# Moving low parts, normalised tiles, sums of results and one set of routed rows from VectorE to GpSimd in a network-attention-network kernel

## What is computed

```python
x = x + 0.5 * ffn(layernorm(x), gate_w, expert_bias, w1, w2, w3)
x = x + attn(layernorm(x), Wq, Wk, Wv, Wo)      # 16 heads of 8, 256 x 256 scores, no mask
x = x + 0.5 * ffn(layernorm(x), gate_w, expert_bias, w1, w2, w3)

def ffn(x, ...):                                  # 8 experts, hidden 352, the best 2 of each token
    scores = softmax(xf @ gate_w.T); _, sel = top_k(scores + expert_bias, 2)
    routed = xf[token_idx] * top_scores_sorted[:, None]       # sorted by expert
    h = silu(routed @ w1[e]) * (routed @ w3[e]); out = h @ w2[e]
    return zeros.at[token_idx].add(out)
```

## Time and profile before

| | us |
|---|---|
| median of 3 runs | 738.89 (738.53 to 741.27) |
| the profiled execution, its own time | 737.8 |
| its span, first to last instruction | 736.0 |
| first network, to the first unit of attention | 0 to about 245 |
| batches 0 to 3 of the attention, from the residual in unit (0, 2) | 248.29 to 317.96 |
| batches 4 to 11, the same way | 317.96 to 441.47 |
| to the last maxima | 471.55 |
| to the first product of the second network | 507.97 |
| second network | to 736 |

### The profile page before, as it was taken

One profiled execution on the slowest core, in us unless ns is written; L12 is line 12 of the kernel. 1 busy time (PEld: TensorE's weight loads), 2 busy tenths in 40 slices (PEclk: granted clock), 3 DMA queues, 4 the chain that ended last, 5 costly groups with the idle time before them and its releaser, 6 DMA issues.

```text
span 736.0 us, 14989 instructions
## 1 busy us (share of the span) xinstructions
PE 621.3 (84%) x5080; PEld 475.7 (65%) x5080; DVE 446.4 (61%) x1164; ACT 390.6 (53%) x912; POOL 303.1 (41%) x312
## 2 busy tenths in 40 slices
PE   6399999999979778899899998899999999999100
PEld 6388999988857434455554554456989899999100
DVE  6955733235456989899999999973676322233211
ACT  1625764444422577778777787783457544444000
POOL 6067714565433373044000010005566077776474
PEclk9999999999999899999999999989999999999655
DMA  8358978787982454435334443016678878887322
GB/s 263 100 165 222 252 225 237 224 239 207 286 231 81 153 147 148 125 117 166 110 116 139 125 130 103 3 58 198 179 211 249 228 218 245 246 250 208 100 78 64
DMA packets 116586, 126.02 MB, mean 171 GB/s; under 512 B 12512, under 2 KB 99168, under 8 KB 116384
## 3 DMA queue, kind: packets, MB, share of 16 engines
q1 hardware_dynamic: 98544, 101.20, 45.7%
q0 software_dynamic: 9088, 18.63, 10.2%
q10 hardware_dynamic: 8880, 5.25, 2.3%
HBM read 89.37 MB, written 35.39 MB: 170 GB/s over the span
## 4 chain that ended last, share of the span: by engine, by line
PE 53%; DVE 24%; issue 6%; DMA 6%; POOL 5%; ACT 4%; SPq 1%; POOLq 0%; ACTq 0%; DVEq 0%
PE banks L684 13%; DVE mx L816 10%; PE banks L656 9%; PE banks L672 8%; PE banks L665 8%; POOL rows L588 4%; PE banks L1128 4%; PE banks L646 2%; PE banks L471 2%; ACT PT L1143 2%; DMA WR<-in_experts 2%; PE banks L1012 2%; PE banks L1101 1%; DVE resid L803 1%; DVE split L809 1%
## 5 line engine op out<-in xcount | busy, mean ns | idle before, releaser
L568 POOL DMA_INDIRECT xe<-routed_rows,idx x156 | 151.6, 972 | 224.7 <-PE banks L646 85.7
L816 DVE TENSOR_REDUCE mx<-banks 128x2 f32<-128x512 f32 x256 | 163.4, 683 | 8.9 <-PE banks L1103 7.7
L1143 ACT ACTIVATE PT<-banks 128x512 f32<-128x512 f32 x256 | 140.5, 604 | 36.4 <-PE banks L1114 34.1
L588 POOL DMA_INDIRECT rows<-slots_out,slot x128 | 124.0, 969 | 72.2 <-issue 27.8
L737 DVE TENSOR_TENSOR hidT<-banks,act 96x256 f32<-96x256 f32 (+1 forms) x92 | 34.9, 380 | 188.2 <-ACT act L718 187.9
L684 PE MATMUL banks<-WR,hidT 128*128 128x128 f32 x936 | 119.8, 275 | 0.6 <-ACT ye L727 0.6
L684 PEld LDWEIGHTS banks<-WR,hidT 128*128 128x128 f32 x936 | 111.9, 191 | 2.9 <-issue 1.0
L656 PE MATMUL banks<-xeT,WR 128*128 128x256 f32 (+1 forms) x368 | 86.1, 356 | 8.0 <-issue 3.8
L672 PE MATMUL banks<-xeT,WR 128*128 128x256 f32 (+1 forms) x368 | 82.8, 347 | 0.0
L665 PE MATMUL banks<-xeT,WR 128*96 128x256 f32 (+1 forms) x368 | 82.5, 347 | 0.0
L1128 PE MATMUL banks<-PT,V 128*32 128x256 f32 x1024 | 73.4, 407 | 4.5 <-ACT oT L1190 3.8
(11 more groups left out here) (160 smaller groups left out, 894.9 us busy)
## 6 DMA issues: line engine op xcount, KB each, us to landing
WR<-in_experts SPq DMA_DIRECT2D x92, 544.0 KB
stacks<-split SPq DMA_DIRECT2D x32, 384.0 KB
slots_out<-ye SPq DMA_DIRECT2D x156, 64.0 KB
QS<-stacks SPq DMA_DIRECT2D x64, 112.0 KB
KS<-stacks SPq DMA_DIRECT2D x64, 112.0 KB
routed_rows<-xn ACTq DMA_DIRECT2D x16, 256.0 KB, 5.3
routed_rows<-xn SPq DMA_DIRECT2D x12, 256.0 KB, 2.3
xe<-routed_rows,idx POOLq DMA_INDIRECT x156, 4.4
```

Source lines behind the costliest of these rows:

```text
L568: eng.indirect_dma_start(xe[:, i % XR, a, :], None, routed_rows[h], bass.IndirectOffsetOnAxis(ap=idx[h][:, tile:tile + 1], axis=0))\
L588: eng.indirect_dma_start(rows[:, k, t, :], None, slots_out[h], bass.IndirectOffsetOnAxis(ap=slot[h][:, k, t:t + 1], axis=0))\
L816: eng.tensor_reduce(mx[:, :, e, pair], maxima_bank(f)[:, :].rearrange("p (q n) -> p q n", q=2), AX.X, ALU.max).then_inc(s_max, 1)
L1143: eng.activation(PT[:, u % 4, 1 - k].rearrange("p t n -> p (t n)"), PS[f % 3], ACT.Exp, scale=scale).then_inc(s_exp2, 1)
```

## The change

Six edits. First, `split_low` for batches 3 to 15 and `normed_pair` for batches 4 to 15 are issued on POOL, in a new function `attention_gpsimd` that follows the units and waits on the exponentials in units 0, 3 and 5. Second, the six sums of results that fall in the attention (chunks 2 and 3 of the first group, all four of the second) are made on POOL (`combine_gpsimd`, two additions of 128x512); DVE keeps their statistics and waits for the sums. Third, the factor 0.5 moves from the sum to ACT's copy of the expert result `ye`, so that a sum is two plain additions on either engine. Fourth, POOL's gathers are issued from the same units and some of them later, the power after two of them. Fifth, the rows for the second choice are made on POOL (`rows_gpsimd`) once the attention's POOL work is done. Sixth, SP stores first- and second-choice rows in turns. A count `s_ready` tells POOL when a reciprocal root is ready.

```diff
-        def rows_vector(eng):
+        def rows_gpsimd(eng):
             eng.wait_ge(s_coef, 2 * 3)
             eng.wait_ge(s_comb, GC * HALVES)
             for t in range(TH):
                 eng.tensor_scalar(rows[:, 1, t, :], X[:, t, :], factor[:, 1, t:t + 1], offset[:, 1, t:t + 1],
                                   ALU.mult, ALU.add).then_inc(s_xv, 1)
-            for k, c in ((0, 0), (0, 1), (0, 2), (1, 0), (0, 3), (1, 1), (1, 2), (1, 3)):
+            for k, c in ((0, 0), (1, 0), (0, 1), (1, 1), (0, 2), (1, 2), (1, 3), (0, 3)):
...
+        def combine_gpsimd(eng, h, c):
+            per = TH // GC
+            eng.wait_ge(s_gath[h][c], 16 * TOP_K * per)
+            eng.wait_ge(s_comb, GC * h + c)
+            a, b = (rows[:, k, c * per:(c + 1) * per, :] for k in range(TOP_K))
+            xc = X[:, h * TH + c * per:h * TH + (c + 1) * per, :]
+            eng.tensor_tensor(a, a, b, ALU.add).then_inc(s_pair, 1)
+            eng.wait_ge(s_pair, GC * h + c - 1)
+            eng.tensor_tensor(xc, a, xc, ALU.add).then_inc(s_comb, 1)
...
-                    eng.copy(ye[:, r, 0:w, :].rearrange("p a d -> p (a d)"), PS[1][:, 0:w * D]).then_inc(s_ye, 1)
+                    eng.activation(ye[:, r, 0:w, :].rearrange("p a d -> p (a d)"), PS[1][:, 0:w * D], ACT.Copy,
+                                   scale=0.5).then_inc(s_ye, 1)
...
+        def attention_gpsimd(eng, *sides):
+            for n in range(BATCH):
+                for u in range(PAIRS):
+                    if u == 2 and n + 3 < BATCH:
+                        split_low(eng, n + 3)
+                    if u == 6 and n + 4 < BATCH:
+                        eng.wait_ge(s_ready, (3, 4, 5, 5, 6, 6)[n // 2])
+                        normed_pair(eng, n + 4)
+                    if u in (0, 3, 5):
+                        wait(eng, s_exp2, 2 * (PAIRS * n + u))
+                    aside(sides, PAIRS * n + u)
+        def first_results(eng, outs):
+            combine_gpsimd(eng, 0, 2)
+            yield
+            next(outs)
+            yield
+            root_gpsimd(eng, 4, 0, tiles_of_chunks(2))
+            for _ in outs:
+                yield
+            combine_gpsimd(eng, 0, 3)
+            yield
+            root_gpsimd(eng, 5, 0, tiles_of_chunks(3))
+            yield
...
+            attention_gpsimd(pool, (first_results(pool, outs), spans((0, 7, 1), (11, 11, 1)), 12),
+                             (second_results(pool), spans((13, 30, 1), (31, 31, 1), (36, 52, 1), (61, 61, 1)), 62),
+                             (third_root(pool), in_loads(90, 1), 90))
+            rows_gpsimd(pool)
...
-            attention_vector(dve, (finish(dve, 4, 0, 2), lambda i: 2 * int(2 <= i <= 4), 5),
-                             (finish(dve, 5, 0, 3), spans((8, 9, 1), (12, 13, 1), (20, 20, 2)), 2 * PAIRS + 5),
+            attention_vector(dve, (finish(dve, 4, 0, 2), spans((1, 3, 1), (4, 4, 2)), 5),
+                             (finish(dve, 5, 0, 3), spans((9, 11, 1), (12, 12, 2)), PAIRS + 5),
```

More of the change, by code:

```diff
@@ L227, in build @@
         s_wa, s_vzero = sem("s_wa"), sem("s_vzero")
+        s_ready, s_pair = sem("s_ready"), sem("s_pair")
         chain = [0]
@@ L261, in norm_sums, with norm_root @@
             yield
-        def norm_root(eng, n, h, t, rstd):
+        def norm_root(eng, n, h, t, rstd, ready=0):
             yield
@@ L270, in norm_root @@
             link(eng, eng.scalar_tensor_tensor(rr[:, t], rr[:, t], -0.5, var[h][:, t], ALU.mult, ALU.mult))
-            link(eng, eng.scalar_tensor_tensor(rstd, rr[:, t], 1.5, rough[h][:, t], ALU.add, ALU.mult))
+            last = eng.scalar_tensor_tensor(rstd, rr[:, t], 1.5, rough[h][:, t], ALU.add, ALU.mult)
+            if ready:
+                last.then_inc(s_ready, 1)
+                eng.wait_ge(s_ready, ready)
+            else:
+                link(eng, last)
             yield
@@ L287, in finish @@
             yield from norm_sums(eng, h, t, amean[:, tiles])
-            yield from norm_root(eng, n, h, t, arstd[:, tiles])
+            yield from norm_root(eng, n, h, t, arstd[:, tiles], n - 1)
         def tiles_of_chunks(*chunks):
@@ L1214, in attention_vector @@
                             largest(eng, f)
-                    if u == 2 and ahead:
-                        split_low(eng, n + 3)
                     if u == 2 and nxt:
```

50 lines of the change are left out of this document (24 added, 26 removed).

## The result

The changed kernel takes 744.21 us (median of 7 runs, 740.79 to 745.49); the kernel before takes 738.89 beside it (7 runs, 734.61 to 741.78). The ratio is 1.0083, 95% interval 1.0047 to 1.0119: slower by some 6 us where 9.4 less were forecast. The profiled execution took 740.79, the shortest of the seven; its span is 739.0, 3.0 longer than before. The stage that the change is about lost more than that. PE had waited there for expert weights in before (1.5 and 1.2 us, at 203.8 and 208.9); in after no such wait between 185 and 237 is over 0.6.

What follows compares the result with a forecast made beforehand. DVE and PE, both nearly full in the attention batches and feeding each other, were taken as the bound. Terms -1.3 + 1.1 + 1.4 + 1.6 + 5.9 + 0.6 + 0.1 gave 9.4 us less, 729.5 from 738.89; range 722.5 to 736.

Steps and rivals of the forecast that it cites:

- Batches 4 to 11: Quiet attention batches: each falls from 15.44 to 14.7 us as work leaves DVE, a gain of 5.9 us.
- The 0.39 behind the low part goes: Unit 2 of a batch: PE's 0.39 us wait for negated maxima behind DVE's low part disappears.
- PE's 14.7: Attention batches: PE, busy 14.08 on average plus 0.6 of remaining waits, sets a batch at 14.7 us.
- DVE and POOL hold each other up: Rival, finishes and final routing: two-input SBUF instructions wait on POOL, 5 to 6 us off the gain; chance 0.12.
- Batch 0: First attention batch: POOL's later gather and sum delay DVE's residual from 268.17 to 269.5, a loss of 1.3 us.
- Batch 1: Second attention batch: PE sets the length, which falls from 16.91 to 15.8 us, a gain of 1.1.
- My 1.1 for the clock: Second attention batch: 1.1 us added to 14.7 for PE's lower granted clock after standing some 4 us.
- Batches 2 and 3: Attention: these go from 16.08 to 14.7 and from 16.80 to 15.2 us, gains of 1.4 and 1.6.
- Batches 12 to 14: Late attention batches: a low part and shorter waits save 0.6 of 30.08 us.
- The end of the attention: Before the second network: first gather at 500.17 instead of 503.24, but PE is occupied, so a gain of 0.1 us.
- PE and ACT hold the period: Rival, attention batches: they stay at 15.1 us, a gain of about 4.6, giving 734; chance 0.15.
- It is wrong if DVE's instructions grow longer: Sign against the forecast, no size given; listed beside DVE waiting for sums in batches 3 to 7 and PE waiting for `xa`.

Runs made afterwards that it cites:

- e3: Changed kernel, with POOL's low part waiting until DVE's negated maxima of that unit are done; ratio 1.0075 to the kernel before.
- e4: Changed kernel, with each maximum taken over half of the keys (128 of 256), leaving out part of the computation; ratio 0.9941 to the kernel before.
- e7: e3 with the root for half of the second group's tiles moved from unit 2 to unit 3 of batch 4; ratio 1.0000 to the kernel before.
- e1: Kernel before, plus a spare 128x512 subtraction on POOL in unit 2 of batches 0 to 12, nothing waiting for it; ratio 1.0190 to the kernel before.
- e9: e7 with DVE's statistics and roots moved to later or roomier units, POOL's first sum waiting for DVE's tiles; 731.20 against 735.40, ratio 0.9929 to the kernel before.
- e6: Changed kernel, with the second-choice rows back on DVE and the stores in the old order; ratio 1.0078 to the kernel before.
- e8: e7 with sums and second-choice rows back on DVE, leaving only low parts and normalised tiles moved to POOL; ratio 1.0041 to the kernel before.
- e5: Changed kernel, with the six late sums of results back on DVE; ratio 1.0162 to the kernel before.

## Why the prediction was wrong

The step that failed is **Batches 4 to 11**, with its gain of 5.9; they lost 4.5 (128.0 for 123.51). "The 0.39 behind the low part goes" is where it breaks. The low part left and the negation behind it grew by 0.51 to 0.70: PE's waits for it went from 5.3 to 6.1 us. The statement that the batch would end at PE's 14.7 was nearly right as a floor (14.87, e3 and e4). The change alone never gets there, since the hold sits on the way. On top came the root of batch 4, held for 1.92, with PE's wait of 2.12 and the fall of its clock behind it (18.05, where e7 with a shorter hold and full clock has 15.61), and batch 7, where the statistics, sums and root stand in one batch (DVE busy 15.17).

**The rival was named and sized wrongly.** "DVE and POOL hold each other up" had a chance of 0.12 and 5 to 6 us. I counted it only for instructions with two operands in SBUF, in the finishes and the routing. I left out the negation, which reads one and runs in every batch: 12 times 0.5 to 0.7, plus what hangs on it. A held instruction costs by its place and by what PE's clock does behind it: holds of 9.4 us cost e1 14 us, and others lie in idle time. The Trainium skill, SBUF - State Buffer, section "Who interferes with whom", says more than the sentence that I had used: a tensor_scalar whose operands meet the conditions can run in a mode with two ports and then contends too, although it reads a single tensor, and whichever engine issued first has the ports for its whole instruction. By that rule the negation is held until POOL's low part ends and the reductions never are; the rows agree on both (0.88 ending with POOL's 1.16; 683 ns before and after). They don't agree for every instruction of POOL: the last section has a power beside which nothing is held.

**Batch 0** was near: 1.3 lost forecast, 0.5 in the trace, with DVE's wait for the sum at 4.23 and the residual 20.36 after the last. **Batch 1** was forecast at 15.8 and took 17.41. My 1.1 for the clock after PE's standing was too little: PE waited up to 4.2 us for the residual there (the value rows, L787), and the clock granted over the batch is 0.80. e9, where DVE's waits ahead of it are gone, has 16.52 and 17.95 for batches 0 and 1, at 0.90. In e9 there is still the held negation of batch 1, with a fall of the clock behind it. **Batches 2 and 3** gained 0.7 and 0.4, not 1.4 and 1.6; e3 gives batch 2 the 14.87. **Ahead of batch 0** there was no term, and 1.1 went: DVE's last pair of tiles was held by POOL's first sum (734 ns each, 1.40 for the pair in e7, where 0.59 was usual), and the first statistics now stand there (0.85). **Batches 12 to 14** were to gain 0.6; from the last residual to the last pair of maxima it is 30.5 for 30.1, 0.4 more. **The end of the attention**: I had the rows 8 us after the coefficients; POOL's waits for exponentials of the last batch stand ahead of them, so that they run from 494.57 to 501.63, up to 24 us after the coefficients (478), and the first gather starts at 506.21, 62.5 after the last residual, where it was 61.8, not earlier. What it costs isn't settled (0.8 in one trace, nothing by e6).

Two places of the working were off by themselves. The stretch of batch 4 from 319.76 to the pair, said to have no idle time of DVE, has 0.28 of it. And the terms given for *PE and ACT hold the period* make 4.1 (2.4 + 3 - 1.3), or 4.8 with the last two of the sum, not 4.6.

**Right** were the prices on POOL: an addition of 128x512 takes 1.27 (1.25 forecast), a low part 1.16. Near them is a tile with 0.79 for 0.5; PE waited for one once, 0.5 us in batch 0. ACT's scaled copy costs nothing that can be seen: from its first product the second network takes 228.0 us (511.00 to 739.0), as before (507.97 to 736.0). "It is wrong if DVE's instructions grow longer" was the sign that came, and PE's waits for `nm`, which were to be gone, with it.

## What to carry to other kernels

Work moved from VectorE to GpSimd isn't free for VectorE if an instruction on two tensors in SBUF, or a small scaling of one, stands beside it there; what reads PSUM was never held here, nor were the statistics, which read SBUF. Look at what VectorE runs in the very microsecond after the moved instruction's input is ready, since both often start on the same event, and put the moved one behind it. Price a hold by what waits behind the held instruction and not by its length, and look at the granted clock behind TensorE's wait: here batches with a fall of it were over 1 us longer than batches with the same hold and none. When an engine is relieved, first measure the floor of the others (halve its work, as in e4): here it was 0.5 below the batch, so that was the most that could be had from a quiet batch, and the rest of the gain lay in moving waits to where there was room.

## Not expected of the hardware

A VectorE instruction on 128x8 elements took 1.92 us in place of 0.17, and one on 128x4 1.15, each beside one GpSimd subtraction of 1.16. One-tensor instructions were held as well: the negation (0.18 to 0.88) and the pair of tiles (0.59 to 1.40). GpSimd's low part wasn't longer for it, 1155 ns on average. But VectorE can hold GpSimd as well: in e8 the low part started at 304.29, beside an addition of VectorE (304.12 to 304.80), and took 1.53; VectorE's next addition, begun at 304.84, took 1.52 for 0.69.

Not everything is held. The statistics read one tensor in SBUF; these four ran beside a GpSimd addition (357.45 to 358.72) and the tiles behind it, at 0.28 each, as alone (changed kernel):

```profile
358.27 0.86 DVE L290 BATCH_NORM_STATS2 stats<-X 128x6 f32<-128x128 f32 x4
```

And not everything holds. In the kernel before, the low part and the negation, the two that were held elsewhere, kept their 0.68 and 0.17 beside a power of GpSimd that reads SBUF too (POOL, then DVE):

```profile
425.67 2.90 POOL L539 TENSOR_TENSOR rough<-var,half_power 128x16 f32<-128x16 f32 x1 [44.33 <-DVE var L260]
```

```profile
427.64 0.68 DVE L809 TENSOR_TENSOR split<-resid,split 128x512 bf16<-128x512 f32 x1
428.24 0.17 DVE L899 TENSOR_SCALAR nm<-mx 128x32 bf16<-128x32 f32 x1
```

A gather on GpSimd can hold too, but shorter and more rarely. In the kernel before, an instruction of the first network that takes 0.17 alone took 0.41 and ended with the gather (77.79):

```profile
76.84 0.95 POOL L568 DMA_INDIRECT xe<-routed_rows,idx  x1 [0.31 <-PE banks L646]
```

```profile
77.38 0.41 DVE L376 TENSOR_SCALAR wrapped<-beyond 128x8 f32<-128x8 f32 x1
```

Of the additions of 128x512 with both inputs in SBUF eight of 16 started beside a gather in that trace, and none took over 696 ns. This bears on both cases of the root (after, 1.92; e3, 1.72): the held instruction started 0.5 to 0.7 us ahead of the low part, while a gather was still being issued (317.75, 1.09 us), and a gather alone held the same kind of instruction in e5 for 0.27 (276.49, 0.43 for 0.16). So the gather seems to have kept it until the low part, 0.03 behind the gather, held it again; the two weren't set apart by a run.
